# Reading of tokens by the landmarks: scores, maxima and exponentials two elements ahead, and half of the zero products

## The reference

```python
l2q = _split_heads(lmf @ w_l2t_q + b_l2t_q).reshape(B, H, Nb, M, DH)
ra = jax.nn.softmax(jnp.einsum('bhnmd,bhnsd->bhnms', l2q, kb) * scale, axis=-1)
ro = jnp.einsum('bhnms,bhnsd->bhnmd', ra, vb)
ro = ro.transpose(0, 2, 3, 1, 4).reshape(B, NL, D)
lmf = lmf + ro @ w_l2t_out + b_l2t_out
```

## Time and profile before

| | us |
|---|---|
| median of 3 runs | 1729.45 |
| lowest and highest | 1728.13, 1736.25 |
| the profiled execution's own time | 1723.58 |
| its span in the trace | 1721.5 |
| PE busy | 1475.1 (86%) |
| DVE busy | 1282.4 (74%) |
| ACT busy | 1002.5 (58%) |
| POOL busy | 578.1 (34%) |

### The profile page before, as it was taken

How to read it: one execution, slowest core, us unless ns; L and a number is a source line. 1 busy time by engine, 2 the same in 40 slices (tenths; PEclk the granted TensorE clock), 3 DMA queues, 4 the chain that set the end, 5 groups by cost and what they waited for, 6 DMA issues and landing times. The chain is left out here.

```text
span 1721.5 us, 30594 instructions
## 1 busy us (share of the span) xinstructions
PE 1475.1 (86%) x11218; PEld 973.8 (57%) x11218; DVE 1282.4 (74%) x2388; ACT 1002.5 (58%) x2539; POOL 578.1 (34%) x600
## 2 busy tenths in 40 slices
PE   2177757999999999999978888699888499999997
PEld 2177735677667766676655766466555144444443
DVE  8999926777777777777734265278887399999996
ACT  7799816877878778877742143277776223333332
POOL 0000004444455445454520000036666433333333
PEclk9555558999999999999987799799999799999999
DMA  2022252323323333323262063446665234444443
GB/s 61 1 59 52 61 167 81 103 91 100 125 94 91 95 104 109 99 91 111 98 208 91 1 207 137 130 131 180 192 174 168 74 80 104 104 99 99 104 99 86
DMA packets 233237, 183.24 MB, mean 106 GB/s; under 512 B 163584, under 2 KB 165248, under 8 KB 233088
## 3 DMA queue, kind: packets, MB, share of 16 engines
q1 hardware_dynamic: 233088, 181.29, 36.8%
HBM read 94.21 MB, written 59.77 MB: 89 GB/s over the span
## 5 line engine op out<-in xcount | busy, mean ns | idle before, releaser
L1054 PE MATMUL al_ps<-w,al_xT 128*128 128x512 f32 (+2 forms) x1024 | 350.6, 496 | 0.0
L1054 PEld LDWEIGHTS al_ps<-w,al_xT 128*128 128x128 f32 x1024 | 191.8, 192 | 126.8 <-issue 107.3
L2204 POOL TENSOR_TENSOR ff_zq<-ff_z,ff_back 128x1024 bf16<-128x1024 fp8e4 x64 | 122.3, 1912 | 225.6 <-DVE ff_z L2227 225.6
L442 PE MATMUL tk_ps<-tk_w,tk_l 128*128 128x64 f32 x512 | 113.0, 422 | 79.4 <-DVE tk_w L411 52.3
L442 PEld LDWEIGHTS tk_ps<-tk_w,tk_l 128*128 128x128 f32 x512 | 110.4, 332 | 82.0 <-issue 82.0
L2171 ACT ACTIVATE ff_sg<-ff_gate 128x1024 f32<-128x1024 f32 x64 | 65.6, 1025 | 148.7 <-PE ff_gate L2250 148.7
L749 POOL TENSOR_TENSOR al_qv<-al_qv,al_qe 128x512 f32<-128x512 f32 x48 | 63.2, 1316 | 234.2 <-PE al_ps L1113 234.2
L2269 PE MATMUL ff_acc<-wdT,ff_zT 128*128 128x512 bf16 x512 | 122.6, 383 | 7.1 <-DMA ff_zT<-ff_zq 7.1
L2250 PE MATMUL ff_up<-wuT,xqT 128*128 128x512 bf16 x512 | 121.7, 381 | 2.8 <-DVE ff_z L2219 2.8
L2250 PE MATMUL ff_gate<-wgT,xqT 128*128 128x512 bf16 x512 | 122.7, 383 | 0.2 <-ACT ff_sg L2171 0.2
L2029 PE MATMUL ag_ps<-ag_w,ag_aT 128*128 128x512 f32 x256 | 114.0, 599 | 1.7 <-ACT ag_ps L1863 1.7
(11 more groups left out here) (294 smaller groups left out, 3284.6 us busy)
## 6 DMA issues: line engine op xcount, KB each, us to landing
al_hx<-h_s SPq DMA_DIRECT2D x36, 256.0 KB, 2.7
o_s<-al_o SPq DMA_DIRECT2D x32, 272.0 KB, 2.2
h_s<-tk_w SPq DMA_DIRECT2D x16, 512.0 KB, 3.8
v_s<-al_v SPq DMA_DIRECT2D x32, 256.0 KB, 2.2
k_s<-al_kT SPq DMA_DIRECT2D x32, 256.0 KB, 2.4
q_s<-al_qT SPq DMA_DIRECT2D x32, 256.0 KB, 2.6
lt_k<-k_s SPq DMA_DIRECT2D x16, 512.0 KB, 4.9
lt_v<-v_s SPq DMA_DIRECT2D x16, 512.0 KB, 3.7
```

Of the source, the lines that this page charges most:

```text
L442: ins = pe.matmul(o, L[:, u, 0, t], R[:, u, t], start=True, stop=True)
L1054: ins = pe.matmul(out, xT[:, T, k], w[:, k, cols], start=False, stop=True, skip_group_check=True)
L2204: pool.tensor_tensor(zq[:, u].rearrange("p (k s) -> p k s", s=QB), z8[:, u].rearrange("p (k s) -> p k s", s=QB), back[:, u, :, None].to_br ...
```

## The change

Three engines' lists are written in another order, and one of the two `stream` calls of each turn is dropped.

- PE: `scores(1)` is issued before the loop; in turn i the scores of i+2 stand where those of i+1 stood. A turn is transposes(i), stream, scores(i+2), sums(i).
- DVE: `maximum(1)` and `queries(2)` come before the loop; a turn is norm(i), queries(i+3), maximum(i+2), pick(i-1).
- ACT: `exp(1)` comes before the loop; a turn is copy(i), exp(i+2).
- `stream` is called once a turn, with two products of zeros, in place of twice.

```diff
@@ scalar
             exp(0)
+            exp(1)
             for i in range(BATCH):
                 copy(i)
-                if i + 1 < BATCH:
-                    exp(i + 1)
+                if i + 2 < BATCH:
+                    exp(i + 2)
@@ vector
             queries(0)
             queries(1)
             maximum(0)
+            maximum(1)
+            queries(2)
             for i in range(BATCH):
                 norm(i)
+                if i + 3 < BATCH:
+                    queries(i + 3)
                 if i + 2 < BATCH:
-                    queries(i + 2)
-                if i + 1 < BATCH:
-                    maximum(i + 1)
+                    maximum(i + 2)
                 if i:
                     pick(i - 1)
             pick(BATCH - 1)
@@ tensor
             scores(0)
+            scores(1)
             for i in range(BATCH):
                 transposes(i)
                 stream()
-                if i + 1 < BATCH:
-                    scores(i + 1)
-                stream()
+                if i + 2 < BATCH:
+                    scores(i + 2)
                 sums(i)
```

## The result

The changed kernel took 1802.54 us (median of 5 runs, 1799.05 to 1804.33) against 1729.45: a ratio of 1.0416, 95% interval 1.0386 to 1.0445. It is slower, by the mechanism forecast, but by 73 us in place of 58, and the time lies 3.5 us above the range given.

The account below looks back on a forecast made before the run. A loop holding one whole key load per turn was taken to bound the stage: 998.85 + 13 x 8.9 + 9.1 = 1123.65 against 1065.39, +58.3 us. Added to the median 1729.45, this gave 1788 us, range 1769 to 1799.

Parts of the forecast that it names:

- This closes a loop that holds one whole key load per turn.: Scores to sums on PE and SP's queue: no key load overlapped by a turn's work, 7.97 us a turn at full clock.
- The load's part, 0.45 + 4.8 + 0.03 = 5.28.: SP to PE, each turn: sums' end to key issue 0.45, issue to landing 4.8, landing to scores 0.03 us.
- At the low clock the last part is longer ... 4.05 in place of 2.69.: PE, scores through sums: 4.05 us at the low clock against 2.69 at full, making a turn of 9.33.
- I take two turns in three.: PE's clock: low in two turns of three, 7.97 + 0.68 x 1.36 = 8.9 us a turn.
- rival (b): Same key loop, PE at low clock in every turn: 9.33 us a turn, +63.9, 1793 us; chance 0.20.
- 998.85 + 13 x 8.9 + 9.1.: Stage's end: end of sums(0), 13 turns, then the last part; 1123.65 against 1065.39, +58.3 us.
- The top of the range: Slow end of the forecast: 1793 with a landing of 5.0, 2.6 more, and a base run of 1736; given as 1799.
- Half of the zeros dropped ... their absence is already in the 2.69.: PE between scores and sums: 32 products, 7 us in all, off the loop before; nothing more to add.
- Rival (c): Key load doesn't bind, being issued early by SP; the loop through DVE stays 4.22 us a turn, -2.6, 1727; chance 0.04.
- the claim that DVE's order would hold the turn at 4.22: Without the key wait, the path maximum, pick, norm, transposes, zeros, scores would bind, 4.22 us a turn.
- Rival (d): Neither keys nor DVE's order bind, PE alone does: 3.48 us a turn, -12.2, 1717 us; chance 0.03.
- What would show it.: Profile signs: stage some 135 us, 13 key waits of 3 to 4, late key issues, PEclk 0.6 to 0.8, DMA share a third.

Follow-up runs that it names:

- e1: Changed kernel with SP's list reordered, the key load of i+2 ahead of the value load of i; 1732.83 us against 1726.96, ratio 1.0032.
- e3: Kernel before with only the second pair of zero products of each turn dropped; 1733.45 us against 1726.96, ratio 1.0040.
- e7: Changed kernel with the second pair of zero products put back between scores and sums; 1802.80 us against 1727.92, ratio 1.0438.
- e5: Changed kernel with key loads issued early and norm(i+1) ahead of maximum(i+2) on DVE; 1719.96 us against 1727.92, ratio 0.9954.
- e8: Kernel before with both stream() calls of the loop deleted; 1741.19 us against 1727.92, ratio 1.0074.
- e2: Changed kernel with 16 zero products after the transposes in place of 2; 1775.04 us against 1726.96, ratio 1.0288.
- e10: Changed kernel with early key loads and norm(i+1) ahead of maximum(i+2), timed again in more rounds; 1720.22 us against 1727.58, ratio 0.9949.
- e4: Kernel before with SP's list reordered, the key load of i+1 ahead of the value load of i; 1723.15 us against 1726.96, ratio 0.9978.
- e6: Changed kernel with early key loads, norm(i+1) ahead of maximum(i+2) and the second zero pair put back; 1714.77 us against 1727.92, ratio 0.9932.
- e11: Changed kernel with early keys, norm(i+1) ahead of maximum(i+2) and all zeros, timed again in more rounds; 1715.34 us against 1727.58, ratio 0.9924.

## Why the prediction was right in kind and wrong in size

*"This closes a loop that holds one whole key load per turn."* Right, shown from both sides: the rows above have it, and e1 takes the load out by SP's list alone and brings the time to within 0.3% of before.

*The load's part, 0.45 + 4.8 + 0.03 = 5.28.* It measured 9.87 - 4.69 = 5.18 on average. The choice between 4.5 and 5.0 was good to 0.1 us.

*"At the low clock the last part is longer ... 4.05 in place of 2.69."* This step failed, and it is the one that puts the time outside the range: with every turn at the 9.33 given here the sum is 1793, inside it. Scores and sums measured 1.01 + 3.68 = 4.69. I took the sums from the earlier trace rows, the first turn, and these rows were not all at the low clock: it came back while they ran, so the weight loads took 2.89 in all where a whole group at 1.2 GHz takes 3.49. The check was in the same rows: 16 records in 2.61 us on PE next to 16 in 1.89 at full clock is a factor of 1.4, where a group wholly at 1.2 GHz, 3.68 to 1.89, has 1.95. Over 13 turns the missing 0.64 us are 8.3 us.

*"I take two turns in three."* This step failed too, in the same direction. It was every turn, worth 0.43 us each or 5.6 in all. I reasoned that the clock falls and comes back within each turn; it never came back, not even in the last two turns, where PE waits for no load. So rival (b) was the true case, but priced at 9.33 it too was short. The Trainium skill, "TensorE: Matmul & The Clock Gate", section "HAM oscillation — how this bites in real kernels", tells of a cold start in every pass of a loop that waits for a DMA. The trace agrees that each pass began at the low clock, but shows no coming and going: the granted clock is 0.50 from 998 us to the end of the stage.

*"998.85 + 13 x 8.9 + 9.1."* By its terms: start +0.4; 13 turns of 9.87 in place of 8.9, of which the products +1.07 and the load -0.10, +12.6; the last part 11.8 in place of 9.1, +2.7. That last part I had taken at the full clock without a reason, and added up wrongly: its own terms, twice 0.7 + 1.34 + 1.9 and then 1.8, give 9.7. Measured, the last two turns are 4.98 each at 1.2 GHz. Together 58.3 + 15.7 = 74.0, which is the stage's difference. But for 0.6 us of adding, what was off is PE at 1.2 GHz: how long its work takes there, and for how many turns. The top of the range was not added up to its end either: 1793 + 2.6 + 6.8 for a base of 1736 is 1802.7, and I wrote 1799.

*"Half of the zeros dropped ... their absence is already in the 2.69."* Off the path in the order before, yes; but not free there: e3 loses 0.4% by it through the clock. In the changed order e7 shows that putting them back saves nothing.

*Rival (c), 1727, and the claim that DVE's order would hold the turn at 4.22.* Its condition was false. e1 makes the condition true: the turns at the full clock are 4.23, as claimed, but the mean is 4.60 and the time 5.9 us above the kernel before, where (c) had 2.6 below it, since it took the clock as full. *Rival (d)* needed two further edits, and e5, which makes them, has a mean turn of 3.44. My 3.48 for PE alone was too long by 0.3: its work takes 3.17 with one pair of zeros, when DVE's is just as long, and 3.51 with both pairs, where DVE has idle time and PE none. That the mean comes near 3.48 is luck, it holds turns that wait for values.

*What would show it.* The key waits, SP's issue times, the stage of some 135 us (151) and the DMA share of a third (0.28) were there. "PEclk between 0.6 and 0.8 with sums of 2.6 beside sums of 1.9" was not.

## What to carry to other kernels

When work is moved ahead on the computing engines, move its loads ahead in the DMA queue too: a load whose own buffer is free can still stand behind another load's wait, and the deeper lead then meets it earlier and not later. Read on every in-order engine what stands between a result and its use; here SP's list and then DVE's each had to be changed before the lead of two was worth anything. Price a low clock from rows that lie in it from end to end, and let the estimate include the case that it stays low through the whole stage.

## What the runs showed of the hardware

PE was hardly idle in e8, by the profile 82.1 of 88.3 us, and yet the granted clock was 0.50 from about 1001 us to the end of the stage, 0.53 in the mean. In e2, with 16 wide zero products a turn, it was 0.94 with PE busy 110.8 of 132.8. In each of the traces looked at (before, after, e1, e8) the first fall came behind the first wait of PE for the norm, 2.2 to 2.6 us long. Later in the stage the clock held with both pairs of zeros and waits of 0.51 us a turn (before); with one pair and waits of 0.85 it fell in some turns and not in others (e1, e3).

The stage in question starts between 985.9 and 994.8 us, though all the work in front of it is identical. Most of this is there already at the first product of `landmark_attention`, which starts between 890.1 and 896.0. What lies ahead of the stage and behind it, together, is 1643 to 1654 us long. These few microseconds are why the totals of e7 and e10 do not follow from their stages alone. In the five traces with two pairs of zeros a turn (before, e4, e6, e7, e11) the stage starts between 987.5 and 988.5, in the eight others anywhere in the wider interval. There is one trace of each kernel, though, and executions of one and the same kernel differ by as much (e5 from 1710.34 us at a mean granted clock of 0.901 to 1730.96 at 0.885), so this may be chance; it was not tried and stays open.
